# Cross-attention and experts: the last step's score tiles on three pairs of banks, two more sums in f16 halves

## What is computed

```python
def reference(x, ctx, ln_m_g, ln_m_b, ln_l_g, ln_l_b, Wq, Wkv, Wout, Wg, W1, b1, W2, b2):
    lat = layer_norm(layernorm(x), ln_l_g, ln_l_b)
    m = layer_norm(ctx, ln_m_g, ln_m_b)
    q = lat @ Wq
    k, v = split(concat([m, lat], axis=1) @ Wkv)
    attn = softmax(q @ k.T / 8)                  # 16 heads, 512 x 666
    x = x + merge_heads(attn @ v) @ Wout
    z = layernorm(x)
    probs = softmax(z @ Wg)
    keep the two largest of 8, scaled to the sum 1 -> scores
    y_e = relu(z @ W1[e] + b1[e]) @ W2[e] + b2[e]
    return x + sum_e(scores_e * y_e)
```

## Time and profile before

| | |
|---|---|
| median of 3 runs | 341.89 us (341.89 to 341.97) |
| the profiled execution | 342.18 us |
| its span, first to last instruction | 340.2 us |
| PE busy | 331.9 us (98%), 2209 matmuls |
| POOL busy | 290.3 us (85%) |
| DVE busy | 272.7 us (80%) |
| ACT busy | 214.8 us (63%) |
| granted TensorE clock | 1.000 |

### The profile page before, as it was taken

The page is one execution under the profiler, slowest core; times in us unless marked ns, Lnnn a source line. Parts: engine busy times, 40 slices in busy tenths (PEclk is TensorE's granted clock), DMA queues, the critical chain, the costliest instruction groups (busy, mean ns, idle before and its releaser), DMA issues.

```text
span 340.2 us, 6018 instructions
## 1 busy us (share of the span) xinstructions
PE 331.9 (98%) x2209; PEld 221.8 (65%) x2209; DVE 272.7 (80%) x413; ACT 214.8 (63%) x305; POOL 290.3 (85%) x188
## 2 busy tenths in 40 slices
PE   7899999999999999999999999999999999999986
PEld 7666666575747565665657584756594548888766
DVE  5989566988989899999898797979737797399494
ACT  2565678584949475675858494957622746487954
POOL 4639999999999999999999999899994899488543
PEclk9999999999999999999999999999999999999999
DMA  4640000000010000000000000000000006100520
GB/s 128 183 129 0 2 0 4 0 17 0 2 31 10 23 2 0 3 1 2 15 2 15 18 0 17 0 2 1 2 0 3 0 0 198 53 2 0 175 106 33
DMA packets 9049, 10.03 MB, mean 29 GB/s; under 512 B 1015, under 2 KB 6061, under 8 KB 9021
## 3 DMA queue, kind: packets, MB, share of 16 engines
q1 hardware_dynamic: 8725, 9.52, 9.0%
q10 hardware_dynamic: 296, 0.13, 0.1%
HBM read 9.09 MB, written 0.56 MB: 28 GB/s over the span
## 4 chain that ended last, share of the span: by engine, by line
PE 93%; issue 2%; ACT 2%; POOL 1%; DVE 1%; POOLq 0%; ACTq 0%; DVEq 0%
PE xo L484 25%; PE sc L464 21%; PE sc L470 6%; PE sc L390 5%; PE sc L391 4%; PE sc L392 4%; PE mx L421 3%; PE xo L421 3%; PE mx L572 2%; PE xo L572 2%; PE xo L493 2%; PE sc L505 2%; PE mx L391 1%; PE mx L390 1%; PE mx L392 1%
## 5 line engine op out<-in xcount | busy, mean ns | idle before, releaser
L1343 POOL TENSOR_TENSOR psum_acc<-psum_acc,probs 111x1024 f32<-111x1024 f32 x64 | 164.0, 2563 | 6.9
L792 ACT ACTIVATE probs<-sc 111x1024 f32<-111x1024 f32 x96 | 98.3, 1028 | 18.5 <-PE sc L470 11.3
L484 PE MATMUL xo<-probs,v_sb 111*64 111x512 f32 x384 | 88.0, 596 | 0.0
L464 PE MATMUL sc<-q_pair,k_pair 64*111 64x512 f32 x576 | 85.9, 401 | 0.8 <-ACT v_sb L782 0.4
L464 PEld LDWEIGHTS sc<-q_pair,k_pair 64*111 64x111 f32 x576 | 44.7, 170 | 28.3 <-issue 11.5
L484 PEld LDWEIGHTS xo<-probs,v_sb 111*64 111x64 f32 x384 | 26.3, 137 | 42.7 <-issue 39.4
L1026 DVE RECIPROCAL recips<-recips 128x128 f32<-128x128 f32 x64 | 54.0, 904 | 0.0
L992 DVE TENSOR_REDUCE part_max<-mx 128x2 f32<-128x888 f32 x32 | 34.7, 1084 | 21.0 <-PE mx L421 19.5
L808 ACT COPY recips<-xo 128x512 f32<-128x512 f32 x16 | 9.4, 587 | 57.5 <-PE xo L493 48.8
L1343 POOL TENSOR_TENSOR psum_acc<-probs 111x1024 f32<-111x1024 f32 x16 | 39.3, 2458 | 7.1 <-ACT probs L792 6.9
L470 PE MATMUL sc<-max_row,ones_r 64*111 64x512 f32 x192 | 38.3, 391 | 0.0
(11 more groups left out here) (241 smaller groups left out, 618.2 us busy)
## 6 DMA issues: line engine op xcount, KB each, us to landing
spread<-score_rows SPq DMA_DIRECT2D x16, 256.0 KB, 5.3
w_raw<-in_L_ffn_W SPq DMA_DIRECT2D x8, 128.0 KB, 2.1
x_tok<-in_x SPq DMA_DIRECT2D x2, 256.0 KB, 3.1
wv_raw<-in_L_xattn_Wkv SPq DMA_DIRECT2D x4, 128.0 KB, 3.4
wout_sb<-in_L_xattn_Wout SPq DMA_DIRECT2D x1, 512.0 KB
wqk_raw<-in_L_xattn_Wq SPq DMA_DIRECT2D x7, 64.0 KB, 1.9
wqk_raw<-in_L_xattn_Wkv SPq DMA_DIRECT2D x7, 64.0 KB, 2.3
out<-x_tok SPq DMA_DIRECT2D x1, 256.0 KB, 2.0
```

Source lines behind the costliest of these rows:

```text
L464: pe.matmul(sc[0:KP, kt % 2, h, :], k_pair[r, s % QKB, k_part, at], q_pair[r, s % QKB, q_part, :], start=(k_part + q_part == 0), stop=False)
L484: mm = pe.matmul(o_ps[h * HD:(h + 1) * HD, :], v_sb[0:KP, s // 2 % 2, kt, at:at + HD], probs[0:KP, e % RING, h, :], start=(kt == 0), stop= ...
L792: act.activation(probs[0:KP, e % RING, :, :], sc[0:KP, kt % 2, :, :], ACT.Exp).then_inc(exp_done, 1)
L1343: pool.tensor_tensor(psum_acc[0:KP, s % 2, :, :], first, probs[0:KP, e % RING, :, :], ALU.add) \
```

## The change

Four things are changed, all from step 13 on.

- HALVED goes from 13 to 15, so the sums of the steps 13 and 14 are made of f16 halves as well. Their `sum_high` and `sum_low` are new: those of step 13 run in step 14 (on DVE before `spread_max`), those of step 14 behind step 14 (on ACT after the copies of W2, on DVE after the norm of x1 and before the reciprocals of step 12).
- The six score tiles of step 15 go round sc[:, 0], sc[:, 1] and xo. A tile waits for the exponentials of three tiles before instead of two; tile 2 also waits for the copies of output 14 and sum 13.
- P.V of step 15 goes to the second bank of sc, the sum of step 14 to the first. The expert halves begin two banks further on, so expert 0 uses the pair sc[:, 1] and expert 1 waits for the copies of sum 14 and output 15. The turn of the scores moves behind expert 1. The sum of step 14 waits for the fourth exponential instead of a copy.
- In `layer_one`, the second half of an expert waits for ACT's relu of two experts ago, where that expert's low part is made by POOL, and no longer for POOL.

```diff
-HALVED = STEPS - 3
+HALVED = STEPS - 1
...
+        def hid(n):
+            return banks_ps[:, (n + 2) % 4, :]
+        def tile_ps(s, kt):
+            return [sc[:, 0], sc[:, 1], xo][kt % 3] if s == STEPS - 1 else sc[:, kt % 2]
+        def sum_ps(s):
+            return [sc[:, 0, 0, :], o_ps][s - STEPS + 2] if s >= STEPS - 2 else pj
+        def out_ps(s):
+            return sc[:, 0, 1, :] if s == STEPS - 1 else o_ps
... in dots(s, kt)
-                if e >= 2:
+                if s == STEPS - 1:
+                    pe.wait_ge(exp_done, s * KT + max(kt - 2, 0))
+                    if kt == 2:
+                        pe.wait_ge(o_copied, s)
+                        pe.wait_ge(sum_copied, s - 1)
+                elif e >= 2:
                     pe.wait_ge(exp_done, e - 1)
... in PE's steps
-                if s > HALVED:
-                    total(s - 1)
                 for kt in range(KT):
-                    if kt == SUM_AT and 1 <= s <= HALVED:
+                    if kt == (SUM_AT if s < STEPS - 2 else 0) and s >= 1:
                         total(s - 1)
... in layer_one(g)
-                    if n < 4:
-                        pe.wait_ge(exp_done, STEPS * KT - (1 if n < 2 else 0))
+                    if n < 2:
+                        pe.wait_ge(exp_done, STEPS * KT - 1)
+                    elif n < 4:
+                        pe.wait_ge(sum_copied, STEPS - 1)
+                        pe.wait_ge(o_copied, STEPS)
                     elif c == 0:
                         pe.wait_ge(r0_done, g - 1)
+                    elif g - 2 in ON_POOL:
+                        pe.wait_ge(r1_done, g - 1)
                     else:
                         second_low(pe, g - 2)
... PE's last step and experts
             logits(0)
-            pe.wait_ge(sum_copied, s - 1)
+            pe.wait_ge(exp_done, s * KT + 4)
             total(s - 1)
...
                 layer_one(g)
-                if g == 0:
+                if g == 1:
                     turn_scores(0)
-                if g == 1:
-                    pe.wait_ge(o_copied, STEPS)
-                    total(s, o_ps)
+                    pe.wait_ge(exp_done, STEPS * KT)
+                    total(s)
                     bias_term(0)
... ACT, in its steps
-                if 2 <= s <= HALVED:
+                if 2 <= s < STEPS - 1:
                     sum_high(s - 1)
...
+                if s == STEPS - 2:
+                    sum_high(s)
... DVE, in its steps and behind them
+                else:
+                    sum_low(s - 1)
                 spread_max(s + 1)
...
             norm_x1(0)
+            sum_low(STEPS - 2)
             for c in range(RC):
                 reciprocal(STEPS - 4, c)
```

More of the change, by code:

```diff
@@ L463, in dots @@
                         r = slice(h * HD, (h + 1) * HD)
-                        pe.matmul(sc[0:KP, kt % 2, h, :], k_pair[r, s % QKB, k_part, at],
+                        pe.matmul(tile_ps(s, kt)[0:KP, h, :], k_pair[r, s % QKB, k_part, at],
                                   q_pair[r, s % QKB, q_part, :], start=(k_part + q_part == 0), stop=False)
@@ L469, in dots @@
                     r = slice(h * HD, (h + 1) * HD)
-                    mm = pe.matmul(sc[0:KP, kt % 2, h, :], ones_r[r, :], max_row[r, s % 2, :],
+                    mm = pe.matmul(tile_ps(s, kt)[0:KP, h, :], ones_r[r, :], max_row[r, s % 2, :],
                                    start=False, stop=True)
@@ L483, in pv, with total @@
                     at = (p % 2) * P + h * HD
-                    mm = pe.matmul(o_ps[h * HD:(h + 1) * HD, :], v_sb[0:KP, s // 2 % 2, kt, at:at + HD],
+                    mm = pe.matmul(out_ps(s)[h * HD:(h + 1) * HD, :], v_sb[0:KP, s // 2 % 2, kt, at:at + HD],
                                    probs[0:KP, e % RING, h, :], start=(kt == 0), stop=(kt == KT - 1))
                 mm.then_inc(pv_done, 1)
-            def total(s, bank=pj):
+            def total(s):
+                bank = sum_ps(s)
                 if s < HALVED:
@@ L791, in exponent @@
                     act.wait_ge(added, (KT - 1) * (r // KT) + max(r % KT, 1))
-                act.activation(probs[0:KP, e % RING, :, :], sc[0:KP, kt % 2, :, :], ACT.Exp).then_inc(exp_done, 1)
+                act.activation(probs[0:KP, e % RING, :, :], tile_ps(s, kt)[0:KP, :, :], ACT.Exp).then_inc(exp_done, 1)
             def copy_output(s):
                 act.wait_ge(pv_done, KT * (s + 1))
-                act.copy(o_t[:, batch_of(s), pair_of(s), :], o_ps[:, :]).then_inc(o_copied, 1)
+                act.copy(o_t[:, batch_of(s), pair_of(s), :], out_ps(s)).then_inc(o_copied, 1)
             def sum_high(s):
@@ L802, in sum_high, with copy_sum @@
                 act.copy(acc_hi[0:KP, :, :], psum_acc[0:KP, s % 2, :, :]).then_inc(acc_hi_done, 1)
-            def copy_sum(s, bank=pj):
+            def copy_sum(s):
                 act.wait_ge(sum_ready, s + 1)
@@ L807, in copy_sum @@
                     act.wait_ge(o_norm, s - 1)
-                act.copy(recips[:, s % 2, :], bank[:, :]).then_inc(sum_copied, 1)
+                act.copy(recips[:, s % 2, :], sum_ps(s)).then_inc(sum_copied, 1)
             act.wait_ge(wqk_loaded[0], 32)
@@ L889, in relu @@
                     act.wait_ge(hid_scaled, n + 1 - SCALED * HC)
-                    act.activation(to, hid_ps[:, n % 4, :], ACT.Relu).then_inc(done, 1)
+                    act.activation(to, hid(n), ACT.Relu).then_inc(done, 1)
                     return
                 act.wait_ge(hid_ready, n + 1)
-                act.activation(to, hid_ps[:, n % 4, :], ACT.Relu,
+                act.activation(to, hid(n), ACT.Relu,
                                bias=cols[:, n % (E * HC):n % (E * HC) + 1]).then_inc(done, 1)
@@ L908, in second_of @@
             def second_of(g):
-                return relu_second_ring[:, g % 2, :] if g in ON_POOL else hid_ps[:, (g * HC + 1) % 4, :]
+                return relu_second_ring[:, g % 2, :] if g in ON_POOL else hid(g * HC + 1)
             def relu_second(g):
@@ L941, in _ @@
                 if g == 1:
-                    copy_sum(STEPS - 1, o_ps)
+                    copy_sum(STEPS - 1)
                 if g in (1, 11):
@@ L1095, in _ @@
                     second_moments()
-                if 1 <= s <= HALVED:
+                if s >= 1 and made:
                     sum_low(s - 1)
-                if 2 <= s <= HALVED:
+                if 2 <= s < STEPS - 2:
                     for c in range(RC):
@@ L1161, in low_second @@
                     dve.wait_ge(y_ready, g - 2)
-                dve.tensor_tensor(relu_lo[:, (g * HC + 1) % FR, :], hid_ps[:, (g * HC + 1) % 4, :],
+                dve.tensor_tensor(relu_lo[:, (g * HC + 1) % FR, :], hid(g * HC + 1),
                                   relu_hi[:, (g * HC + 1) % FR, :].bitcast(F32), ALU.subtract).then_inc(lo1_done, 1)
@@ L1171, in scale_hidden @@
                     dve.wait_ge(spread_in[e], 16 * B)
-                    bank = hid_ps[:, n % 4, :]
+                    bank = hid(n)
                     dve.scalar_tensor_tensor(bank, bank, cols[:, n % (E * HC):n % (E * HC) + 1], spread[:, e, :],
```

4 lines of the change are left out of this document (2 added, 2 removed).

## The result

The changed kernel takes 346.07 us (median of 4 runs: 344.06, 348.12, 343.92, 348.08) against 341.93 before. The ratio is 1.011, with a 95% interval of 1.006 to 1.017. The prediction was 342.2, with a range up to 342.9. The kernel is slower, clear of noise, and outside the range.

The account below looks back on a forecast made before the run. TensorE, holding 93% of the chain of waits, was taken as the bound, with POOL 0.41 us behind. Net +0.6 us up to expert 2 less 0.3 at the end gave +0.3 on 341.89: 342.2 us, range 341.3 to 342.9.

Parts of the forecast that it names:

- Part 1: Sums of steps 13 and 14 in f16 halves: PE saves 0.48 us twice, POOL's last addition comes 1.0 us later.
- rival C: Step 14's last POOL addition ends too late for rstd, adding 0.4 us to POOL's chain: 342.9 us, 12%.
- Part 2: Last step's scores on three pairs of banks: waits between tiles go, PE gains 0.9 us, 1.1 at most.
- Part 3: Other banks for P.V, step 14's sum and the experts: no instruction added, new waits covered by PE's work on expert 0.
- The sum up to sum 15: PE arrives 1.86 us sooner but waits 2.6 us for POOL's last addition: net +0.6 us where expert 2 begins.
- the 0.1 us that was to come back: The last sum, stretched to 1.01 us by the bias term's wait for scores, would shorten because scores come early.
- Part 4: Experts' second bank waits for ACT's relu, not POOL: the 1.26 us stall near the end goes, end gains 0.3 us.
- The clock behind the wait: After PE's 2.6 us wait before the last sum, the total counted PE's work without any clock term.
- rival D: PE's 2.6 us idle time drops the clock to 1.2 GHz, doubling 3.5 us of work behind it: 345.7 us, 5%.
- The sign that I named: Forecast wrong if the end moves over 0.4 us against expert 2, PE doesn't wait at the last sum, or rstd passes 259.1.
- The shared port pair: DVE subtraction beside POOL additions in step 14: 1.09 us on POOL by the trace, 1.22 by the skill's lock rule.

Follow-up runs that it names:

- part 1 alone: The kernel before with only the sums of steps 13 and 14 in f16 halves, with their new copies and subtractions: 344.17 us, ratio 1.005.

## Why the prediction was wrong

What PE did before the last sum, how often the clock fell, and what the kernels took:

| kernel | idle before the last sum, profiled execution | executions with a clock of 0.995 or less | median us |
|---|---|---|---|
| before | none there; 1.26 near the end | 0 of 68, taken beside the experiments | 341.9 to 342.1 |
| changed, sum 14 in f32, norm 13 late | none | 0 of 6 | 340.57 |
| changed, both sums in f32, norm 13 late | none | 0 of 7 | 340.81 |
| changed, eleven matmuls | none | 0 of 12 | 342.63 |
| changed, f32 sums, norm 13 as before | 0.57 | 0 of 12 | 341.73 |
| changed, subtraction and norm 13 late | 0.57 | 0 of 11 | 341.41 |
| changed, subtraction on POOL | 0.81, and 1.27 earlier | 2 of 11 | 342.44 |
| before, part 1 alone | 1.61 | 4 of 6 | 344.17 |
| changed, four matmuls | 1.63 | 8 of 10 | 344.34 |
| changed, subtraction late | 1.65 | 6 of 6 | 344.58 |
| before, W2 ahead of the last addition | 2.25 | 4 of 4 | 348.42 |
| changed | 2.49 and 2.45 | 9 of 10 | 346.07 and 345.62 |

The experiments were run on three chips, each beside the kernel before. On every one of them the clock fell in kernels with 1.6 us or more of idle time before the last sum and not in those with none or 0.57 us, so the chip is not the cause.

- **Part 1, right in mechanism and size.** The sums saved about 0.46 us each, the subtraction of step 14 put the reciprocals of step 12 1.14 us later, and the normalisation started at 265.47 (+0.25 for the start) against 265.72. The additions of step 14 took 8.17 us, less than the 8.4 to 8.5 named: the subtraction cost POOL 0.79 us, not 1.09. rstd did not become late, though its idle time shrank to 0.34 us; rival C did not occur.
- **Part 2, right.** The tiles took 267.73 - 262.00 = 5.73 us against 6.69, a gain of 0.96 where I had 0.9. The logits did not wait. Part 3 cost nothing either: expert 1 follows expert 0 without a gap.
- **The sum up to sum 15, right but for 0.1.** 2.6 us of waiting was forecast and 2.49 measured. Expert 2 came 0.7 us later, where I had 0.6: the 0.1 us that was to come back did not, because the last sum again took 281.41 - 280.40 = 1.01 us, although the bias term's scores were copied out by 278.5.
- **Part 4, wrong in size.** I took 0.3 us for the end, and it was 0.08; of the stall that was to go, 0.55 us stayed in the changed kernel. I compared the start of the last matmul, 336.30, plus a guessed remainder, with the modelled end of the old one, 336.66; with its start, near 336.38 (the second of the two that begin at 336.26), the difference would have been 0.08. Hence the change costs 0.6 us without the clock, where I had 0.3, and the kernel with eleven matmuls, 342.63 against 341.94, bears that out within its interval.
- **The clock behind the wait: this is the step that failed.** The sum has no term for it, so it takes PE's work behind its own idle time of 2.6 us at full clock. That idle time was the condition of rival D, and I gave D 5%, with the range ending at 342.9, far below D's 345.7. I argued from the fact that nothing fell behind the 1.26 us stall, and no row spoke for 2.6. An untested state is no evidence for its being harmless. The fall happened in 9 of 10 executions. Its price was not the one of 3.5 us that I gave: 1.56 us in the profiled execution, and about 5.5 in those near 348 (348.1 - 341.9, less the 0.7 of waiting), with others between (345.6 to 345.8 at a mean clock of 0.99). That the median, 346.07, lies near D's 345.7 is luck: it is the middle between runs near 344 and runs near 348. (C and D together are 17%, not the 15% given for a slower kernel.) The sign that I named did show it: the end moved by 1.5 us against expert 2 (57.07 us from there to DVE's last instruction, against 55.58), not by less than 0.4. The kernel before with 2.25 us of idle time shows the same mechanism (0.50 at 283 us). The Trainium skill (TensorE: Matmul & The Clock Gate, Part 1) states it: idleness brings 1.2 GHz and activity 2.4. The traces agree; what was wrong was the chance.
- **The shared port pair, right in direction.** A subtraction with two SBUF inputs took 3.14 us beside POOL's additions instead of 1.22, and two of these took 0.8 us more. The prediction's block of 1.22 us was too long: POOL's additions lost 0.79 us in step 14 and 0.8 us here. DVE's norm, a tensor_scalar with one tensor input, took 2.91 us instead of 1.11 beside a POOL subtraction of 2.13 us; one of its four pieces took 2.15 us, the others 0.34. The Trainium skill (SBUF — State Buffer, "SBUF: two separate sides") has the rule: such a subtraction, or a DVE instruction in a 2-port mode, and a GpSimd instruction shut each other out. The rows agree in direction; none shows whether the norm ran in such a mode.

What stays open: which executions fall for 3.4 us, which for longer, and which not at all. The same program did all three, by its mean clocks. Where between 0.57 and 1.6 us of idle time the falls begin was not tested (two kernels lie between, with 2 of 11 and with 0 of 68, but their idle times stand elsewhere). And of the runs near 348 no profile exists.

## What to carry to other kernels

When an edit makes the bounding engine wait for a second one, work out the length of the wait and price the clock with it as a case of its own, even if the time of the edit itself comes out even. Here a net loss of 0.7 us became one of 2 to 6 us in most executions. Filling the wait with matmuls whose result nobody uses got most of it back, and shortening the POOL chain that caused it (one normalisation moved behind the last addition, one extra subtraction left out) turned a loss of 1.1% into a gain of 0.5%.

Before moving work into the idle time of VectorE or GpSimd, look at what the other of the two runs then.

## What was not expected of the hardware

The clock need not be low while PE stands idle: in the changed kernel it was 1.00 through the wait (277.9 to 280.4) and for 2.7 us of matmuls behind it, and fell at 283.1. Of the five profiled falls four came 1.5 to 2.7 us after the last sum had started, and one, in the kernel before with W2 moved, 0.2 us ahead of it. A reader who looks for the fall inside the gap alone will mostly not find it. And a single execution of a kernel of this kind says little: the unedited changed kernel took from 343.64 to 348.12 us, while the kernels without the idle time spread over 0.6 to 1.4 us.
